# Edge count of a graph layer: compares over 750 (destination, source block) pairs and a final turn by TensorE, in place of compares over all 1250 sources

## The chip, the cores and the metric

The kernel runs on one core of a Trainium2 chip. The metric is device time in microseconds (us) of one launch. Three runs of the kernel before took 2452.61, 2454.36 and 2455.51 us, median 2454.36 us. The core has five engines that matter here, each with its own instruction queue: PE (TensorE, matmuls, with its weight loads shown as PEld), DVE (VectorE), ACT (ScalarE), POOL (GpSimd) and SP (which issues DMAs). They meet at semaphores.

## The reference, cut to what matters

The program is four layers on 1250 nodes with 512 features: graph attention, mixture of experts, message passing, a spline network. Only the first is touched:

```python
K = (x @ Wk + bk).reshape(N, HEADS, DK)          # N = 1250, HEADS = 8, DK = 32
Q = (x @ Wq + bq).reshape(N, HEADS, DK)
V = (x @ Wv + bv).reshape(N, HEADS, DV)
att = jnp.exp(jnp.einsum('ehd,ehd->eh', Q[receivers], K[senders]) / sqrt(DK))   # 21250 edges
denom = jax.ops.segment_sum(att, receivers, num_segments=N)
att = att / denom[receivers]
msg = att[:, :, None] * V[senders]
agg = jnp.zeros((N, HEADS, DV), dtype=V.dtype).at[receivers].add(msg)
```

`receivers` and `senders` come from `edge_index = stack([src, dst])`, so the sum runs over each node's outgoing edges. The edges are sorted by `dst`. An edge may occur more than once, so what the layer needs of the graph is a dense matrix count[dst, src], 1250 x 1250: how many edges there are from each source to each destination.

## The kernel before, in words

The kernel is written engine by engine in blocks. A block ends when every engine has come to its end; then the next block's instructions start. Inside a block the order on each engine is the order of the code, and nothing but semaphores ties the engines. No planner is in it.

The first block of `attention` is the one that changes. It does this:

1. DVE makes small tables from the edge lists (`unit_ranges`, lines 199 to 248) while PE computes the node means (line 400). DVE waits there for a maximum over partitions by POOL (line 189). Then DVE centres x (486), ACT squares (451), PE takes the variance (406), ACT and DVE make the scale and apply it (454, 490, 492).
2. PE multiplies the result with Wq, Wk, Wv in 22 pieces, 12 for q and k (line 389) and 10 for v (line 393). ACT and DVE take them out of PSUM (446, 475, 481). Eight pieces come ahead of the count, the others are spread over it (`GROUPS`).
3. The count. The 21250 edges are 170 tiles of 125 edges, in 43 units of 4 tiles (`TU`). The destinations are 10 blocks of 125. For each block b a loop runs over the units that may hold its destinations, with bounds that `block_range` loads from a table at run time. Since a unit can lie in two blocks, the loops make 52 turns in all, 208 tiles. For each tile DVE writes two one-hot matrices in f16:

```python
dve.tensor_scalar(dst1[:, q, :], c.iota16[:, b * B:b * B + B],          # line 502, 125 x 125
                  c.dstF[:, bass.ds(u * TU + q, 1)], None, ALU.is_equal)
ins = dve.tensor_scalar(src1[:, q, :], c.iota16[:, 0:N],                # line 504, 125 x 1250
                        c.srcF[:, bass.ds(u * TU + q, 1)], None, ALU.is_equal)
```

PE multiplies dst1 (stationary) with src1 (moving, three matmuls of 512, 512 and 226 columns, line 427) and sums in PSUM over all tiles of the block, between matmuls with zeros that open and close the sum (420, 432). DVE may be one loop turn ahead of PE. At the end of a block ACT copies the 125 x 1250 sums into `count[:, b, :]` and takes their row sums on the way (`deg`, line 460), and PE goes on to the next block only when that is done (`s_out`).

The next block of the program loads q and k from memory (`stack`, on SP) and starts the scores (line 593). `count` is used there by DVE. A later stage (message passing, lines 1343 to 1449) has already an edge loop of the kind that the change uses here: windows over destinations per unit, `unit_windows` (lines 119 to 121) for the table loads, one-hots by ACT (1444, 1449), a sum by PE (1357) that DVE adds to an accumulator (1399). Line 1222 is a matmul of f32 data as the stationary operand with an identity as the moving one.

## Time and profile before

| what | us |
|---|---|
| median of three runs | 2454.36 |
| the profiled execution | 2449.78 |
| its span (first to last instruction) | 2448.1 |
| PE busy in the span | 2158.8 |
| DVE busy | 1373.3 |
| ACT busy | 1051.4 |
| POOL busy | 575.8 |
| first compare of the count starts at | 76.92 |
| last count copy by ACT starts at | 269.05 |
| first score matmul of the next block at | 284.72 |

How to read it: all starts are us from the span's start. A row of a timeline has the start, the length, the engine, the line of the code, the operation, the names of what it writes and reads, the shape, how many instructions were merged into the row, and in brackets how long the engine had been idle before it and who ended that. The length of an instruction runs a little into the next one's on DVE and PE, which are pipelined, so the distance between starts is shorter than the length. A f32 matmul shows as two matmul instructions, each with a weight load of its own. DVEq and PEldq are instructions that an engine's sequencer does by itself (loads of a register, arithmetic on it, branches).

### The profile page before, as it was taken

The page shows a single profiled execution, that of the slowest core. Times are in us where ns is not written, and L with a number is a line of the kernel's source. Part 1 is how long each engine was busy: PE and PEld are TensorE (multiplying, and loading weights), DVE is VectorE, ACT ScalarE, POOL GpSimd, SP SyncE. Part 2 cuts the span into 40 slices and gives each one's busy share as a digit, 9 for nine tenths or more (in the row PEclk, how much of TensorE's full clock was granted, in tenths as well). Part 3 has the DMA queues.
Part 4 walks back from the last instruction along what each step waited for, and adds up shares of the span by engine and source line. Part 5 has one row for each costly group of instructions (what it writes and reads, how often), then busy time and mean ns, then how long its engine had stood idle before and what let it go on. Part 6 is the DMA issues. An engine that isn't in the chain of part 4 may idle for free. (4 is left out here: it accounts for less than half of the span.)

```text
span 2448.1 us, 36182 instructions
## 1 busy us (share of the span) xinstructions
PE 2158.8 (88%) x12773; PEld 1662.3 (68%) x12773; DVE 1373.3 (56%) x1922; ACT 1051.4 (43%) x1402; POOL 575.8 (24%) x527
## 2 busy tenths in 40 slices
PE   6898699778949999999995786999999995899998
PEld 2455344355539999999994735999855553799998
DVE  5577577434226666666660053555412127999997
ACT  1100266121016666666660014777601114766665
POOL 1000100001742222222215606888500004000000
PEclk9999899878969999999997898999999997999999
DMA  2100340112038888888874525788520003000001
GB/s 104 51 8 0 84 99 18 36 56 94 2 95 267 283 279 281 282 285 283 282 241 129 148 70 159 205 202 205 152 91 0 0 0 155 1 1 1 0 0 43
DMA packets 111369, 287.13 MB, mean 117 GB/s; under 512 B 48070, under 2 KB 55221, under 8 KB 101536
## 3 DMA queue, kind: packets, MB, share of 16 engines
q1 hardware_dynamic: 45536, 195.78, 24.4%
q0 software_dynamic: 65728, 89.97, 13.9%
q8 instruction: 63, 1.03, 0.2%
q14 instruction: 42, 0.34, 0.0%
HBM read 239.16 MB, written 43.65 MB: 116 GB/s over the span
## 5 line engine op out<-in xcount | busy, mean ns | idle before, releaser
L1832 PE MATMUL ps<-ft,kw 128*128 128x125 f32 x2880 | 342.1, 279 | 37.4 <-DVE ft L1757 24.3
L1832 PEld LDWEIGHTS ps<-ft,kw 128*128 128x128 f32 x2880 | 330.0, 193 | 51.6 <-DVE ft L1757 31.1
L1142 DVE TENSOR_TENSOR wl<-wexp,wh 128x2048 fp32r<-128x2048 f32 (+1 forms) x128 | 225.0, 1759 | 162.3 <-ACT wh L1064 162.3
L1016 PE MATMUL ps<-xh,wh 128*128 128x234 f32 x1024 | 287.6, 281 | 2.2 <-DVE xl L1155 2.2
L1016 PE MATMUL ps<-xh,wl 128*128 128x234 f32 x1024 | 283.3, 277 | 0.0
L1016 PE MATMUL ps<-xl,wh 128*128 128x234 f32 x1024 | 282.9, 276 | 0.0
L1326 POOL DMA_INDIRECT pg<-prows,srcI x170 | 216.6, 1274 | 54.6 <-issue 39.5
L1064 ACT ACTIVATE wh<-wexp 128x2048 fp32r<-128x2048 f32 (+1 forms) x128 | 190.9, 1492 | 63.2 <-DVE gates L1135 63.2
L1016 PEld LDWEIGHTS ps<-xh,wh 128*128 128x128 f32 x1024 | 197.7, 193 | 2.6 <-DVE xl L1155 2.6
L1016 PEld LDWEIGHTS ps<-xh,wl 128*128 128x128 f32 x1024 | 198.4, 194 | 0.0
L1016 PEld LDWEIGHTS ps<-xl,wh 128*128 128x128 f32 x1024 | 198.1, 193 | 0.0
L1357 PEld LDWEIGHTS ps<-ehot,msg 125*128 125x128 f32 x1360 | 160.9, 195 | 11.7 <-issue 5.9
L1357 PE MATMUL ps<-ehot,msg 125*128 125x125 f32 x1360 | 161.8, 278 | 6.9 <-ACT ehot L1449 5.7
L983 POOL DMA_INDIRECT xg<-nrows,idn x128 | 141.1, 1102 | 76.5 <-POOL idn L979 53.7
L1781 ACT ACTIVATE ksq<-ksrc,kn 128x750 f32<-128x750 f32 (+2 forms) x144 | 116.5, 813 | 97.4 <-DVE cube L1740 97.4
L427 PE MATMUL ps<-src,dst 125*125 125x512 f16 (+1 forms) x624 | 133.7, 357 | 17.9 <-DVE src L504 17.9
L1701 POOL COPY ksrc<-nT 128x500 f32<-128x500 f32 (+1 forms) x10 | 10.7, 1074 | 518.9 <-SPq L1692 279.5
L427 PEld LDWEIGHTS ps<-src,dst 125*125 125x125 f16 x624 | 76.1, 141 | 74.8 <-DVE src L504 44.4
L1740 DVE SCALAR_TENSOR_TENSOR cube<-ksrc,kn,ksq 128x750 f32<-128x750 f32 (+2 forms) x144 | 124.7, 880 | 2.6 <-ACT ksq L1781 0.9
L1435 ACT ACTIVATE msg<-epre 125x1024 f32<-125x1024 f32 x85 | 89.8, 1057 | 61.0 <-DVE epre L1389 56.6
L504 DVE TENSOR_SCALAR src<-iota,srcF 125x1250 f16<-125x1250 f16 x208 | 112.6, 541 | 0.0
L1389 DVE TENSOR_TENSOR epre<-ps,pg 125x1024 f32<-125x1024 f32 x85 | 102.3, 1221 | 11.3 <-DMA pg<-prows,srcI 8.6
(256 smaller groups left out, 4009.9 us busy)
## 6 DMA issues: line engine op xcount, KB each, us to landing
wexp<-wexp_d SPq DMA_DIRECT2D x64, 1024.0 KB, 7.3
wexp<-wexp_d SPq DMA_DIRECT2D x64, 512.0 KB, 6.6
yrows<-y SPq DMA_DIRECT2D x64, 468.0 KB
attr<-attr_d SPq DMA_DIRECT2D x42, 250.0 KB, 5.1
kw<-kw_d SPq DMA_DIRECT2D x2, 4608.0 KB, 19.0
qs<-qk SPq DMA_DIRECT2D x32, 156.2 KB, 5.5
ks<-qk SPq DMA_DIRECT2D x32, 156.2 KB, 5.7
qk<-qkhl SPq DMA_DIRECT2D x16, 256.0 KB, 2.4
```

The source lines that it names most:

```text
L427: mm = pe.matmul(c.psf[0:B, a:a + w], dst1[:, q, :], src1[:, q, a:a + w], start=False, stop=False, skip_group_check=True)
L504: ins = dve.tensor_scalar(src1[:, q, :], c.iota16[:, 0:N], c.srcF[:, bass.ds(u * TU + q, 1)], None, ALU.is_equal)
L983: pool.indirect_dma_start(xg[:, q, h, :], None, d["nrows"], bass.IndirectOffsetOnAxis(ap=idn[:, q, h:h + 1], axis=0)).then_inc(s_g[q], 16)
L1016: mm = pe.matmul(c.ps[:, 2 + 2 * s + w, m * CAP:m * CAP + CAP], lhs[:, s, a:a + P], rhs[:, s, k, :], start=(k == 0 and n == 0), stop=(k == ...
L1064: act.activation(wh[:, s, part], wexp[:, s, part], ACT.Copy).then_inc(to, 1)
L1142: dve.tensor_tensor(wl[:, s, part], wexp[:, s, part], wh[:, s, part].bitcast(F32), ALU.subtract)\
L1326: pool.indirect_dma_start(pg[:, p % 4, t % 2, :], None, d["prows"], bass.IndirectOffsetOnAxis(ap=c.srcI[:, t:t + 1], axis=0)).then_inc(s_g ...
L1357: mm = pe.matmul(c.ps[:, ACC, m * W:m * W + W], msg[:, u % 2, q, m * P:m * P + P], hot[:, q, :], start=(q == 0), stop=(q == last))
L1389: dve.tensor_tensor(pre[:, p % 3, :, :], c.ps[0:B, at:at + 2, :], pg[:, p % 4, :, :], ALU.add)\
L1740: dve.scalar_tensor_tensor(cube[:, j % RT, cs], x, kcol(NEG, j), sq[:, j % 2, cs], ALU.add, ALU.mult).then_inc(s_cube, 1)
L1781: act.activation(sq[:, j % 2, cs], x, ACT.Square, bias=kcol(NEG, j)).then_inc(s_sq, 1)
L1832: mm = pe.matmul(out[:, m * B:m * B + B], w[:, k, f, m * P:m * P + P], ft[:, f % RF, a:a + B], start=False, stop=False, skip_group_check=True)
```

## The change

The count is made the other way round. Instead of a sum per block of destinations over all 1250 sources, each unit, now of 8 tiles (`TC`, 22 units, the last with 2 tiles), makes its own small sum and adds it to a table.

The table `pairs` has 125 rows, the place of the source in its block of 125, and 12500 columns, one for each pair (destination, source block), at 10 times the destination plus the block. For each tile DVE writes one one-hot over 750 pairs (75 destinations from the unit's first one, 10 blocks), `row1`; ACT writes the one-hot of the place, `low1`, by a square and a relu of a distance. PE multiplies them (512 and 238 columns) and sums over the unit's 8 tiles; DVE adds the 125 x 750 sum to the table at an offset known at run time. If a unit's destinations reach over more than 75, the loop goes round again for the next 75, for which DVE lowers `rel` by 750; for the given edges every one of the 22 units reaches over 13 to 62 destinations, so that each loop goes round once. At the end PE turns the table: for each of the 10 destination blocks and each of the 10 source blocks a f32 matmul has 125 columns of the table, 10 elements apart, as its stationary operand and the identity as its moving one (12 matmuls a block, since two of them are cut at a PSUM bank's edge). ACT copies the result over the same place, `count`, with the row sums as before.

The table `pairs` is set to zero by POOL (125 x 13250, f32). The v and q/k pieces that lay between blocks now lie one by one ahead of units 1 to 14 on PE, and behind their adds on DVE. In `unit_ranges` the bounds of the blocks are gone; new are the block and place of each edge's source (11 small DVE instructions of 125 x 176 ahead of the wait for POOL) and a second set of window tables. The attention itself and all later stages are the same.

```diff
+TC = 8
+UC = -(-T // TC)
+WC, SH10 = 75, NB
+CW = WC * SH10
+NWC = -(-N // WC)
...
-def block_range(c, eng, b):
-
-
-    lo = eng.value_load(c.tab[0:1, b:b + 1], min_val=0, max_val=U - 1)
-    hi = eng.value_load(c.tab[0:1, NB + b:NB + b + 1], min_val=1, max_val=U)
-    off = eng.value_load(c.tab[0:1, 2 * NB + b:2 * NB + b + 1], min_val=0, max_val=U * NB + U)
-    return lo, hi, off
+def count_windows(c, eng, u):
+
+    base = eng.value_load(c.ctab[0:1, u:u + 1], min_val=0, max_val=N - 1)
+    count = eng.value_load(c.ctab[0:1, UC + u:UC + u + 1], min_val=1, max_val=NWC)
+    before = eng.value_load(c.ctab[0:1, 2 * UC + u:2 * UC + u + 1], min_val=0, max_val=UC * NWC)
+    return base, count, before
...
+        then(dve.tensor_scalar(sh[:, :], srcF[:, :], float(B), None, ALU.is_ge))
+        for j in range(2, NB):
+            then(dve.scalar_tensor_tensor(sh[:, :], srcF[:, :], float(j * B), sh[:, :], ALU.is_ge, ALU.add))
+        then(dve.scalar_tensor_tensor(c.slN[:, :], sh[:, :], float(B), srcF[:, :], ALU.mult, ALU.subtract))
+        then(dve.scalar_tensor_tensor(sh[:, :], dstF[:, :], float(SH10), sh[:, :], ALU.mult, ALU.add))
...
+        first = hi_c[:, 1, :].rearrange("p (u o) -> p u o", o=1).broadcast_to([B, UC, TC])
+        then(dve.scalar_tensor_tensor(by_unit(c.rel[:, :]), first, float(SH10), by_unit(sh[:, :]), ALU.mult, ALU.add))
+
+        def windows(table, units, top, neg, steps, hits, number):
+
+            a = lambda t: t[0:1, 0:units]
+            then(dve.tensor_scalar(a(low), neg, -1.0, None, ALU.mult))
+            then(dve.tensor_tensor(a(reach), top, a(low), ALU.subtract))
+            spread = a(reach).rearrange("p (o u) -> p o u", o=1).broadcast_to([1, number, units])
+            then(dve.tensor_tensor(hits[:, :, :], spread, steps[:, :, :], ALU.is_ge))
+            then(dve.tensor_reduce(a(cnt), hits[:, :, :].rearrange("p b u -> p u b"), AX_X, ALU.add))
+            then(dve.memset(a(one), 1.0))
+            then(dve.tensor_tensor_scan(a(pre), a(one), a(cnt), 0.0, ALU.mult, ALU.add))
+            then(dve.tensor_tensor(a(pre), a(pre), a(cnt), ALU.subtract))
+            dve.tensor_copy(table[:, 0:units], a(low))
+            dve.tensor_copy(table[:, units:2 * units], a(cnt))
+            then(dve.tensor_copy(table[:, 2 * units:], a(pre)))
+
+        windows(c.ctab, UC, hi_c[0:1, 0, :], hi_c[0:1, 1, :], thrc, cc, NWC)
+        windows(c.utab, U, hi_u[0:1, 0, :], hi_u[0:1, 1, :], thr, c1, NB)
...
-        count = sm("count", [B, NB, N], F32)
+        table = sm("pairs", [B, N * SH10 + CW], F32)
+        count = table[:, 0:N * SH10].rearrange("p (b n) -> p b n", b=NB)
...
-        sizes = (8, 2, 2, 2, 2, 2, 1, 1, 1, 1)
-        GROUPS = [range(sum(sizes[:b]), sum(sizes[:b + 1])) for b in range(NB)]
+        GROUPS = [range(0, 8)] + [range(7 + u, 8 + u) for u in range(1, 15)] + [range(0)] * (UC - 15)
...
+            low1 = sf("low1", [B, 2, TC, B], F16)
+            row1 = sf("row1", [B, TC, CW], F16)
+            dist = sf("fdist", [B, TC, B], F32)
...
+                pool.memset(table[:, :], 0.0).then_inc(s_zero, 1)
...
+                pe.wait_ge(s_tab, 1)
+                for u in range(UC):
+                    for r in GROUPS[u]:
+                        piece(r)
+                    base, number, n = count_windows(c, pe, u)
+                    last = len(tiles_of(u)) - 1
+                    pe.wait_ge(s_low, u + 1)
+                    with pe.Fori(0, number) as k:
+                        for q in range(last + 1):
+                            if q % 2 == 0:
+                                pe.wait_ge(s_row, n * full + k * halves(u) + q // 2 + 1)
+                            for a, w in ((0, 512), (512, CW - 512)):
+                                mm = pe.matmul(c.psf[0:B, a:a + w], low1[:, u % 2, q, :], row1[:, q, a:a + w],
+                                               start=(q == 0), stop=(q == last))
+                        mm.then_inc(s_seg, 1)
+                pe.wait_ge(s_ev, len(PIECES))
+                pe.wait_ge(s_add, n + number)
                 for b in range(NB):
-                    for r in GROUPS[b]:
-                        piece(r)
-                    if b == 0:
-                        pe.wait_ge(s_tab, 1)
-                    else:
-                        pe.wait_ge(s_out, b)
-                    lo, hi, off = block_range(c, pe, b)
-                    for a, w in SPANS:
-                        pe.matmul(c.psf[0:B, a:a + w], c.zero16[0:1, 0:B], c.zero16[0:1, 0:w],
-                                  start=True, stop=False, skip_group_check=True)
-                    with pe.Fori(lo, hi) as u:
-                        for h in range(TU // 2):
-                            pe.wait_ge(s_hot, (u + off) * 2 + h + 1)
-                            for q in (2 * h, 2 * h + 1):
-                                for a, w in SPANS:
-                                    mm = pe.matmul(c.psf[0:B, a:a + w], dst1[:, q, :],
-                                                   src1[:, q, a:a + w], start=False, stop=False,
-                                                   skip_group_check=True)
-                            mm.then_inc(s_free, 1)
-                    for a, w in SPANS:
-                        mm = pe.matmul(c.psf[0:B, a:a + w], c.zero16[0:1, 0:B], c.zero16[0:1, 0:w],
-                                       start=False, stop=True, skip_group_check=True)
-                    mm.then_inc(s_full, 1)
+                    if b >= 2:
+                        pe.wait_ge(s_out, b - 1)
+                    for g in range(SH10):
+                        nodes = table[:, b * N:b * N + N].rearrange("p (n g) -> p g n", g=SH10)[:, g, :]
+                        for a, end in parts(g):
+                            mm = pe.matmul(turned(b)[:, a:end], nodes, c.ident[0:B, a - g * B:end - g * B],
+                                           start=True, stop=True, skip_group_check=True)
+                    mm.then_inc(s_turn, 1)
...
+                act.wait_ge(s_tab, 1)
+                for u in range(UC):
+                    m = len(tiles_of(u))
+                    if u:
+                        act.wait_ge(s_low, u)
+                    for q in range(m):
+                        ins = act.activation(dist[:, q, :], c.iota16[:, 0:B], ACT.Square,
+                                             bias=c.slN[:, u * TC + q:u * TC + q + 1])
+                    ins.then_inc(s_dist, 1)
+                    act.wait_ge(s_dist, u + 1)
+                    if u >= 2:
+                        done = act.value_load(c.ctab[0:1, 2 * UC + u - 1:2 * UC + u], min_val=1, max_val=UC * NWC)
+                        act.wait_ge(s_seg, done)
+                    act.activation(low1[:, u % 2, 0:m, :], dist[:, 0:m, :], ACT.Relu, scale=-1.0,
+                                   bias=c.one[0:B, 0:1]).then_inc(s_low, 1)
+                    for r in GROUPS[u]:
+                        high(r)
                 for b in range(NB):
-                    for r in GROUPS[b]:
-                        high(r)
-                    act.wait_ge(s_full, b + 1)
-                    act.activation(count[:, b, :], tile_sum(c, 0, B), ACT.Copy,
-                                   accum_out=c.deg[:, b:b + 1]).then_inc(s_out, 1)
+                    act.wait_ge(s_turn, b + 1)
+                    act.activation(count[:, b, :], turned(b), ACT.Copy, accum_out=c.deg[:, b:b + 1]).then_inc(s_out, 1)
...
-                for r in GROUPS[0]:
-                    evict(r)
-                for b in range(NB):
-                    lo, hi, off = block_range(c, dve, b)
-                    with dve.Fori(lo, hi) as u:
-                        for h in range(TU // 2):
-                            dve.wait_ge(s_free, (u + off) * 2 + h + 1)
-                            for q in (2 * h, 2 * h + 1):
-                                dve.tensor_scalar(dst1[:, q, :], c.iota16[:, b * B:b * B + B],
-                                                  c.dstF[:, bass.ds(u * TU + q, 1)], None, ALU.is_equal)
-                                ins = dve.tensor_scalar(src1[:, q, :], c.iota16[:, 0:N],
-                                                        c.srcF[:, bass.ds(u * TU + q, 1)], None, ALU.is_equal)
-                            ins.then_inc(s_hot, 1)
-                    if b:
-                        for r in GROUPS[b]:
+                dve.wait_ge(s_zero, 1)
+                for u in range(UC):
+                    if u == 0:
+                        for r in GROUPS[0]:
+                            evict(r)
+                    base, number, n = count_windows(c, dve, u)
+                    tiles = tiles_of(u)
+                    with dve.Fori(0, number) as k:
+                        dve.wait_ge(s_next, n + k + 1)
+                        for q, t in enumerate(tiles):
+                            ins = dve.tensor_scalar(row1[:, q, :], c.iota16[:, 0:CW], c.rel[:, t:t + 1], None,
+                                                    ALU.is_equal)
+                            if q % 2:
+                                ins.then_inc(s_row, 1)
+                        dve.wait_ge(s_row, n * full + (k + 1) * halves(u))
+                        cols = c.rel[:, tiles[0]:tiles[-1] + 1]
+                        dve.tensor_scalar(cols, cols, -float(CW), None, ALU.add).then_inc(s_next, 1)
+                        dve.wait_ge(s_seg, n + k + 1)
+                        at = table[:, bass.ds(c.nc.s_assert_within((base + k * WC) * SH10, 0, N * SH10 - SH10), CW)]
+                        dve.tensor_tensor(at, at, c.psf[0:B, 0:CW], ALU.add).then_inc(s_add, 1)
+                    if u:
+                        for r in GROUPS[u]:
                             evict(r)
```

Where the instructions stand now, without times. First DVE, the count's loop in the kernel before, from its entry (`tab` is the table of block bounds, `dst` and `src` the one-hots):

```order
L113 TENSOR_LOAD tab
L113 ISA x2
L498 UNCONDITIONAL_BRANCH
L498 ISA
L502 ISA
L502 TENSOR_SCALAR dst<-iota,dstF 125x125
L504 REGISTER_ALU
L504 TENSOR_SCALAR src<-iota,srcF 125x1250
```

and the same place of the changed kernel, one whole unit and the table loads of the next one (`row` is the one-hot over pairs, `rel` the edges' pair numbers, `pairs` the table):

```order
L528 UNCONDITIONAL_BRANCH
L528 ISA
L531 TENSOR_SCALAR row<-iota,rel 125x750 x8
L535 ISA
L537 TENSOR_SCALAR rel<-rel 125x8
L539 ISA x2
L540 ISA
L540 TENSOR_TENSOR pairs<-pairs,ps 125x750
L528 REGISTER_ALU
L528 COMPARE_AND_BRANCH
L115 TENSOR_LOAD ctab
L115 ISA x2
```

What moved: two compares a tile became one without register work ahead of it, and an add to the table that waits for PE now stands at the end of every unit, ahead of the next unit's table loads (three, of which the first is shown).

Second PE, a loop turn of the kernel before with its end (`zero` closes the sum in PSUM):

```order
L424 REGISTER_ALU
L427 MATMUL ps<-src,dst 125x512 x2
L427 MATMUL ps<-src,dst 125x226
L427 MATMUL ps<-src,dst 125x512 x2
L427 MATMUL ps<-src,dst 125x226
L422 REGISTER_ALU
L422 COMPARE_AND_BRANCH
L432 MATMUL ps<-zero 125x512 x2
L432 MATMUL ps<-zero 125x226
```

and of the changed kernel the last unit's two tiles and the first of the ten blocks of the turn:

```order
L434 MATMUL ps<-row,low 125x512
L434 MATMUL ps<-row,low 125x238
L429 REGISTER_ALU
L429 COMPARE_AND_BRANCH
L438 REGISTER_ALU
L445 MATMUL ps<-ident,pairs 125x125 x4
L445 MATMUL ps<-ident,pairs 125x12
L445 MATMUL ps<-ident,pairs 125x113
L445 MATMUL ps<-ident,pairs 125x125 x3
L445 MATMUL ps<-ident,pairs 125x24
L445 MATMUL ps<-ident,pairs 125x101
```

What moved: the zero matmuls are gone, a tile has two matmuls instead of three, and 120 f32 matmuls (10 blocks of 12) stand behind the last unit.

## Rows read from the trace of the kernel before

**Rows 1.** The page, busy us with share of the span and instructions.

```profile
PE 2158.8 (88%) x12773; PEld 1662.3 (68%) x12773; DVE 1373.3 (56%) x1922; ACT 1051.4 (43%) x1402; POOL 575.8 (24%) x527
```

**Rows 2.** Busy time by stretches: us, PE, PEld, DVE, ACT, POOL, PEclk, DMA share, GB/s.

```profile
76.00:271.00 195.00, 171.24 (x793) 102.46 (x793) 138.43 (x430) 15.20 (x25) 0.00 (x0) 0.97 0.02 7
271.00:285.00 14.00, 0.28 (x1) 0.31 (x2) 0.00 (x0) 0.90 (x1) 6.63 (x3) 0.58 0.99 212
```

**Rows 3.** Waits from 76 to 271: total us, times, longest us.

```profile
DVE dst L502 <- PE ps L427: 52.0, 54, 3.9
```

**Rows 4.** The large compares from 76 to 271: busy us, mean ns, idle before.

```profile
L504 DVE TENSOR_SCALAR src<-iota,srcF 125x1250 f16<-125x1250 f16 x208 | 112.6, 541 | 0.0
```

**Rows 5.** Timeline of DVE: the first compare, and across a block's end.

```profile
76.92 0.26 DVE L502 TENSOR_SCALAR dst<-iota,dstF 125x125 f16<-125x125 f16 x1 [2.05 <-issue]
...
247.24 0.26 DVE L502 TENSOR_SCALAR dst<-iota,dstF 125x125 f16<-125x125 f16 x1
247.41 0.54 DVE L504 TENSOR_SCALAR src<-iota,srcF 125x1250 f16<-125x1250 f16 x1
247.86 0.25 DVE L502 TENSOR_SCALAR dst<-iota,dstF 125x125 f16<-125x125 f16 x1
...
248.48 0.41 DVE L481 TENSOR_TENSOR vs<-ps,par 125x256 f32<-125x256 f32 x1
249.97 0.26 DVE L502 TENSOR_SCALAR dst<-iota,dstF 125x125 f16<-125x125 f16 x1 [1.08 <-PE ps L427]
```

**Rows 6.** Lines 498 and 111 there: ns minimum, median, maximum, first and last start.

```profile
L498 DVEq ALU_OP  x2: 40/40/40, 247.6 to 250.9; - x2
...
L111 DVEq TENSOR_LOAD <-tab x1: 316/316/316, 247.8 to 247.8; - x1
```

**Rows 7.** Timeline of PE in the count.

```profile
193.38 0.73 PE L420 MATMUL ps<-zero 1*125 1x512 f16 x3 [1.40 <-issue]
194.04 5.07 PE L427 MATMUL ps<-src,dst 125*125 125x512 f16 x18
...
233.30 2.35 PE L427 MATMUL ps<-src,dst 125*125 125x512 f16 x12
```

**Rows 8.** Timeline of DVE in the tables ahead of the mean.

```profile
17.56 0.50 DVE L211 TENSOR_REDUCE acc<-acc 1x86 f32<-1x344 f32 x1 [11.17 <-POOL acc L189]
...
22.06 0.59 DVE L224 TENSOR_REDUCE acc<-acc 1x10 f32<-1x430 f32 x1
...
25.60 0.18 DVE L238 TENSOR_SCALAR acc<-acc 1x43 f32<-1x43 f32 x1
...
26.66 0.91 DVE L242 TENSOR_REDUCE acc<-acc 1x43 f32<-1x430 f32 x1
...
28.88 2.29 DVE L486 TENSOR_TENSOR nT<-xT,ps 128x2048 f32<-128x2048 f32 x1 [0.26 <-DVE utab L248]
```

**Rows 9.** Timeline of PE at line 1222, identity times f32 data.

```profile
1337.06 7.25 PE L1222 MATMUL ps<-ident,part 125*128 125x125 f32 x48 [3.79 <-DMA part<-yrows,kidx]
1345.81 5.62 PE L1222 MATMUL ps<-ident,part 125*128 125x125 f32 x48 [1.49 <-DMA part<-yrows,kidx]
...
1364.34 7.25 PE L1222 MATMUL ps<-ident,part 125*128 125x125 f32 x48 [2.13 <-DMA part<-yrows,kidx]
```

**Rows 10.** The message passing stage: a sum by PE and the add behind it.

```profile
1508.94 3.73 PE L1357 MATMUL ps<-ehot,msg 125*128 125x125 f32 x32
...
1513.14 0.68 DVE L1399 TENSOR_TENSOR ST<-ST,ps 128x500 f32 x1 [2.78 <-PE ps L1357]
```

**Rows 11.** Timeline of ACT, one-hots of that stage, and the last count copy.

```profile
269.05 1.21 ACT L460 ACTIVATE count<-ps 125x1250 f32<-125x1250 f32 x1 [17.14 <-PE ps L432]
...
1512.56 1.27 ACT L1444 ACTIVATE edist<-iota,dstN 125x125 f32 x4 [0.59 <-issue]
1513.86 0.72 ACT L1449 ACTIVATE ehot<-edist,one 125x500 f32<-125x500 f32 x1
```

**Rows 12.** POOL's memset at line 1321: ns minimum, median, maximum, first and last start.

```profile
L1321 POOL MEMSET ST<- x1: 4681/4681/4681, 1478.3 to 1478.3; 128x5500 f32 x1
```

More of the change, by code:

```diff
@@ L197, in then @@
             dve.wait_ge(s_step, done[0])
-        dve.memset(c.dstF[:, :], -1.0)
-        dve.memset(c.srcF[:, :], -1.0)
+        dve.memset(dstF[:, :], -1.0)
+        dve.memset(srcF[:, :], 0.0)
         dve.memset(c.dstN[:, :], 1.0)
@@ L229, in dve_part @@
-        for b in range(1, NB):
-            a = 2 * NB + b
-            then(dve.tensor_tensor(tabf[:, a:a + 1], tabf[:, a - 1:a], cnt[:, b - 1:b], ALU.add))
-        then(dve.tensor_tensor(tabf[:, 2 * NB:], tabf[:, 2 * NB:], lo[:, :], ALU.subtract))
-        then(dve.tensor_copy(tabf[:, 0:NB], lo[:, :]))
-        then(dve.tensor_copy(tabf[:, NB:2 * NB], hi[:, :]))
-        then(dve.tensor_copy(c.tab[:, :], tabf[:, :]))
-        top, low = hi_u[0:1, 0, :], hi_u[0:1, 1, :]
-        then(dve.tensor_scalar(ublo[:, :], low, -1.0, None, ALU.mult))
@@ L347, in attention @@
             hl = sf("qkhl", [P, HL, 2, 512], F32R)
[L348 to L352 removed]
+            low1 = sf("low1", [B, 2, TC, B], F16)
+            row1 = sf("row1", [B, TC, CW], F16)
+            dist = sf("fdist", [B, TC, B], F32)
+            s_wqkv, s_mean, s_cent, s_sq, s_var, s_std, s_rstd, s_norm, s_mm, s_hi, s_ev, s_tab, s_dist, \
+                s_low, s_row, s_seg, s_add, s_next, s_zero, s_turn, s_out = (c.sem("fr_" + n) for n in (
+                    "wqkv", "mean", "cent", "sq", "var", "std", "rstd", "norm", "mm", "hi", "ev", "tab", "dist", "low",
+                    "row", "seg", "add", "next", "zero", "turn", "out"))
             s_st = [c.sem(f"fr_st{i}") for i in range(HL)]
```

80 lines of the change are left out of this document (32 added, 48 removed).

## The prediction

> **What bounds the kernel now.** I went from the page's busy shares to a table by stretches, then to the waits, and last to timelines of single engines in the stretch that changes. PE is busy for 88% of the span [rows 1], but the change touches only the first 285 us, so that share says little. In the stretch of the count, 76 to 271, PE is busy for 171 of 195 us and DVE for 138 [rows 2]. Behind it the program has 14 us in which PE has next to nothing, because the next block's loads begin only when this block is over [rows 2]. So whatever end the count stage has, the rest of the program hangs on it one for one, and a reader can treat the stage's last instruction as the end that counts. It is ACT's last copy, 269.05 to 270.3 [rows 11].
>
> Inside the stage two engines share the work. DVE spends 0.17 us from a small compare to the large one and 0.45 from the large to the next small one (247.24, 247.41, 247.86) [rows 5], 0.62 a tile, and 208 tiles [rows 4] make 129 us; DVE's idle time ahead of its compares is put down to PE, 52 us [rows 3], part of it the loop's own turn. PE takes a unit of four tiles, 12 matmuls, in 2.35 us when nothing holds it (233.30) [rows 7], 0.59 a tile. The two alternate closely, and each block end adds a copy by ACT that PE waits for: PE stands idle 1.40 us ahead of line 420 [rows 7]. The stage is thus some 193 us (76.92 to 270.3) for 52 loop turns and 10 ends.
>
> **The change, part by part.**
>
> *The tables ahead of the mean.* DVE waits for POOL until 17.56, and then its own chain runs to 28.88, where the centring starts [rows 8]; PE is done with the mean before that, so this chain sets the start of everything. The 11 new instructions on 125 x 176 stand ahead of the wait, in 11.17 us of idle time [rows 8]; they cost nothing. Behind it the chain was 11.3 us. New: the reduction of 86 again (0.53), one of 125 x 352 (0.55, as the 0.50 of 344 elements), one of 176 elements for `rel` (0.3), a first window table with 374 elements where the old one has 430 (2.95 by the 3.28 from 25.60 to 28.88), and the old one (3.28). That is 7.6 us, 3.7 less. The first compare moves from 76.92 [rows 5] to 73.2, since pieces and evictions between are unchanged. Bounds: 3 to 4.5 us.
>
> *POOL's memset.* 5500 elements take 4.68 us [rows 12], so 13250 take 11.3; begun at 17.5, where DVE's wait for POOL ends [rows 8], they are over at 29, and the first add is at 77. Hidden, with 48 us to spare.
>
> *A unit: the compares and the sum.* A compare of 1250 and one of 125 take 0.45 and 0.17 us of DVE, so 0.25 ns an element, and one of 750 takes 0.33. Each pair of tiles frees PE. PE's tile is 1250 columns in 0.59 us now, 750 in 0.35. The two are about equal. From a unit's first compare: the first pair is ready at 0.33 + 0.41 + 0.06 = 0.8, then PE's 8 tiles take 2.8, and 0.2 goes into drain and waits: 3.8 us. Bounds 3.5 (DVE alone sets it) to 4.3 (a wait shown at each of four pairs).
>
> *A unit: the add and the next start.* This is serial and new. The add waits for the unit's last matmul. In the stage that has the like, PE's group ends at 1512.67 and the add starts at 1513.14, 0.47 later, with two waits and an address to work out [rows 10]; here one wait fewer, I take 0.25 (bounds 0.1 and 0.47). Behind the add come the loop's end and three table loads: in the trace of before the loop's last ALU operation is at 247.6, the first load at 247.8 [rows 6], the next compare at 249.97 [rows 5], 2.35 us in all. Before, this was hidden, since DVE was a turn ahead of PE and its queue still held a compare and an eviction (248.48) [rows 5]. Now the loads begin only when the add has been issued, and the add itself (0.94 us for 750 elements, by the 0.68 for 500 [rows 10] and about one ns for each more) and the eviction (0.41) run beside them. So a unit costs 3.8 + 0.25 + 2.35 = 6.4 us. Evictions are free, and so are the pieces on PE: 2 us right behind the sum, in a hole of 3.4.
>
> *ACT.* Four squares take 1.27 us and a relu of 500 0.72 [rows 11], so 8 squares and a relu of 1000 some 3.6 to 3.9 with a table load, against 6.4 a unit, and one unit ahead by the double buffer. It costs nothing.
>
> *The clock.* The granted clock of PE falls to its lower level (1.2 GHz) where PE has pauses: at line 1222 a group of 48 takes 5.62 us after a pause of 1.49, and 7.25 after pauses of 3.79 and 2.13 [rows 9], 1.63 more. In the count itself 18 matmuls took 5.07 us after a pause of 1.40 [rows 7]. From unit 15 on no piece fills the hole and PE pauses 3.4 us in every 6.4. I charge 1.65 for each of units 15 to 20, and 1.6 for the first unit, which is slow in before too. Units 1 to 14, with 1.4 to 1.8 of pause, I leave warm. Bounds: 0 for all of them, and 14 x 1.65 = 23 more.
>
> *The turn.* 120 f32 matmuls are 240 instructions, each with its weight load. The same operation, data as the stationary operand and identity as the moving one, takes 5.62 / 48 = 0.117 us [rows 9] where the data are contiguous. Here its 125 columns lie 40 bytes apart. No PE row of before shows that. The nearest row is DVE's: a reduction of 430 contiguous f32 takes 0.59 us and one of 430 that lie 172 bytes apart 0.91 [rows 8]. It is not the number of results, for 344 elements with 86 results take 0.50 [rows 8]. With 0.14 of fixed cost (0.59 at 1.04 ns each) the strided read is 1.79 ns an element. 125 of these are 0.224 us, twice what a load has now, and a weight load that long can't hide behind a matmul of 125 columns. Ends: 240 x 0.117 = 28.1 us and 240 x 0.224 = 53.8. I take the upper one, since the slowdown is shown on reads of the same memory and PE asks for elements faster than DVE. ACT's copies (1.3 each against 5.4 a block) hide but for the last one, 1.4.
>
> The Trainium skill speaks against the change here: "SBUF — State Buffer", section "Door 1: The DMA port swizzle", says that accesses that leave a 16-byte line each time pay a penalty, so that four f32 is as far as one strides for free. The trace agrees for DVE, 1.79 against 1.04 ns. The other way points "TensorE: Matmul & The Clock Gate", section "LDWEIGHTS (loading the stationary operand)": a load takes its number of columns divided by 1.2 GHz, 0.104 us for 125, with no term for the stride; line 1222's 0.117 agrees for contiguous data, and by it the turn would stay at the lower end.
>
> *The sum.* First compare 73.2; unit 0 3.8 + 1.6 = 78.6; units 1 to 14 14 x 6.4 = 168.2; units 15 to 20 6 x 8.05 = 216.5; unit 21 with two tiles 2.6 + 0.8 + 1.5 = 221.4; last add 1.3, 222.7; turn 53.8, 276.5; last copy 1.4, 277.9. Before it was 270.3, so the stage ends 7.6 us later. The profiled execution would go from 2449.8 to 2457.4; it lies 4.6 below the median of the runs, which goes from 2454.4 to 2462.
>
> **The rivals.**
>
> *A: the stride is free on PE.* Then the turn is 28.1 + 1.6 (it starts at the low clock) and the stage ends at 253.8, 16.5 us earlier: 2438. For it: 170 tiles in place of 208, and one compare where there were two; the only row of this operation on PE shows 0.117. Against: rows 8. This is the case of a clear gain.
>
> *B: the stride costs, but PE's clock stays high from unit 15 on.* 9.9 us less than my sum: 2452, no difference. For it: the clock held through most of the count, 0.97 [rows 2]. Against: pauses of 3.4 us, after which line 1222 was slow each time.
>
> *C: the clock falls in units 1 to 14 too.* PE then needs 1.65 more in each, 23 in all: 2485 with the stride's cost, 2461 without. For it: the 5.07 us after a pause of only 1.40 [rows 7]. Against: 1.49 without a loss [rows 9]. It decides by how the clock answers to the 1.4 to 1.8 us of pause behind each piece, which the two rows leave open.
>
> The other side for me is A (faster). It decides by the weight load alone: 222.7 + 1.4 + 240 loads reach 270.3 at 0.193 us a load, a gain of 4.9 us at 0.172 and a loss of 4.9 at 0.213.
>
> **How the numbers follow.** I give my forecast 0.56, A 0.30, B 0.08, C 0.06. Within 0.2%, 4.9 us, is what a measurement of this kernel can't tell from no change. My forecast has 7.6 us with an own range of 2454 to 2472 (a unit at 6.1 to 6.8 is minus 6 to plus 8), so some three quarters of it are slower and nearly all the rest is the same; A is faster but for a sliver; B is the same or a bit slower; C slower mostly. Faster 0.32, same 0.20, slower 0.48. The range goes down into A until 2435 and up to 2474.
>
> **What would show it.** Right: first compare near 73; 22 groups of compares about 6.4 us apart, 8 in the last seven full ones, with the table loads of DVE between add and compare; weight loads of the turn starting 0.22 us apart; the turn 54 us long; ACT's last copy near 277. Wrong: turn loads 0.12 apart (A), a granted clock of 1.00 from unit 15 on (B), groups over 7.5 us apart from the start (C), or compares that begin less than 2 us behind the add, by which my serial term would be too large.

## The result and the profile after

| | before | after |
|---|---|---|
| median us | 2453.49 (4 runs, 2452.43 to 2455.51) | 2475.97 (4 runs, 2469.93 to 2481.02) |
| profiled execution | 2449.78 | 2469.93 |
| its span | 2448.1 | 2468.2 |
| end of ACT's last count copy | 270.3 | 287.1 |

The change makes the kernel slower, by a little and clear of the spread: ratio 1.009, 95% interval 1.0063 to 1.0116. I had forecast 2462.0 in a range up to 2474. The direction held; the time is out of the range by 2 us. Two single executions are left out of all ratios, one of the kernel before at 5631.01 us and one of a kernel below at 9319.67 us; nothing recorded says what held them.

The page still says that PE is nearly all of the span, as in [rows 1]:

```profile
PE 2138.6 (87%) x12669; PEld 1678.7 (68%) x12669; DVE 1334.2 (54%) x1719; ACT 1126.8 (46%) x1594; POOL 587.3 (24%) x528
```

PE and DVE are busy for less time than before and the kernel is slower, so the loss isn't in the amount of their work but in when it can be done. Timelines of DVE (first four rows) and POOL (last two) in the tables ahead of the mean, which answer to [rows 8]; the columns are those of the rows ahead of the prediction:

```profile
17.81 0.34 DVE L229 SCALAR_TENSOR_TENSOR rel<-acc 125x176 f32<-125x176 f32 x1
18.18 11.74 DVE L234 TENSOR_SCALAR acc<-acc 1x22 f32<-1x22 f32 x1
29.96 0.17 DVE L235 TENSOR_TENSOR acc<-acc 1x22 f32<-1x22 f32 x1
...
35.86 5.49 DVE L513 TENSOR_TENSOR nT<-xT,ps 128x2048 f32<-128x2048 f32 x3 [0.26 <-DVE utab L244]
```

```profile
16.50 11.22 POOL L373 MEMSET pairs<- 125x13250 f32 x1
27.58 2.31 POOL L374 MEMSET vs<- 125x2560 f32 x1
```

An operation on 22 numbers took 11.74 us. It ends at 29.92, and POOL's second memset ends at 29.89. No semaphore ties the two; the hold doesn't show as idle time but as the length of the instruction, so no view of waits lists it. Ahead of it two reductions and line 229 ran at their usual length beside the same memset. The centring, at 28.88 in [rows 8], starts at 35.86.

A unit in the middle of the count, timeline of DVE (against [rows 5]), and DVE's table loads there with ns minimum, median, maximum, first and last start (against [rows 6]):

```profile
156.41 2.70 DVE L531 TENSOR_SCALAR row<-iota,rel 125x750 f16<-125x750 f16 x8 [0.97 <-issue]
...
160.43 0.94 DVE L540 TENSOR_TENSOR pairs<-pairs,ps 125x750 f32 x1 [1.11 <-PE ps L434]
161.28 0.42 DVE L508 TENSOR_TENSOR vs<-ps,par 125x256 f32<-125x256 f32 x1
162.69 1.39 DVE L531 TENSOR_SCALAR row<-iota,rel 125x750 f16<-125x750 f16 x4 [0.99 <-issue]
```

```profile
L115 DVEq TENSOR_LOAD <-ctab x1: 309/309/309, 160.6 to 160.6; - x1
```

```profile
L117 DVEq TENSOR_LOAD <-ctab x2: 297/305/313, 155.6 to 161.9; - x2
```

From first compare to add 4.02 us, from add to the next compare 2.26, a unit 6.28. The first load (160.6) comes behind the add's issue and the third at 161.9. PE from unit 14 to unit 17, and its turn, which has no counterpart before:

```profile
176.04 2.81 PE L434 MATMUL ps<-row,low 125*125 125x512 f16 x16 [1.74 <-DVE row L531]
182.29 2.81 PE L434 MATMUL ps<-row,low 125*125 125x512 f16 x16 [3.44 <-DVE row L531]
188.54 5.26 PE L434 MATMUL ps<-row,low 125*125 125x512 f16 x16 [3.44 <-DVE row L531]
197.21 4.44 PE L434 MATMUL ps<-row,low 125*125 125x512 f16 x16 [3.41 <-DVE row L531]
...
232.52 53.26 PE L445 MATMUL ps<-ident,pairs 125*125 125x125 f32 x240 [1.40 <-DVE pairs L540]
```

```profile
L445 PEld LDWEIGHTS ps<-ident,pairs x240: 298/315/321, 232.5 to 285.3; 125*125 125x125 f32 x120
```

After two pauses of 3.44 us a group costs 4.2 to 5.3 us in place of 2.81; the granted clock is 1.00 from 150 to 176 and 0.70 from 188 to 230. The turn's 240 loads start (285.3 - 232.5) / 239 = 0.221 us apart, nearly twice the 0.117 of [rows 9]. ACT's last copy answers to the first of [rows 11]:

```profile
285.81 1.21 ACT L488 ACTIVATE pairs<-ps 125x1250 f32<-125x1250 f32 x1 [3.89 <-PE ps L445]
```

Of the span's 20.1 us, 16.8 stand at this copy's end. The other 3.3 lie behind it, where nothing was changed: 2181.1 us from there to the end, against 2177.8. In the profiles of the experiments the same stretch takes 2178.9 to 2184.8, so before's profiled execution was one of its shortest, and the 3.3 lie within what unchanged code varies by.

### The profile page after: what moved, and what is told of

Read it like the earlier page. It is cut to its first block and busy times, and to the rows that moved or that the text cites. A ratio compares the mean times of both kernels' runs of the same rounds, so it can differ in the third digit from the quotient of the medians.

```text
span 2468.2 us, 35717 instructions
## 1 busy us (share of the span) xinstructions
PE 2138.6 (87%) x12669; PEld 1678.7 (68%) x12669; DVE 1334.2 (54%) x1719; ACT 1126.8 (46%) x1594; POOL 587.3 (24%) x528
## 5 line engine op out<-in xcount | busy, mean ns | idle before, releaser
L1360 POOL DMA_INDIRECT pg<-prows,srcI x170 | 216.5, 1274 | 53.1 <-issue 39.5
L1391 PEld LDWEIGHTS ps<-ehot,msg 125*128 125x128 f32 x1360 | 159.7, 193 | 11.6 <-issue 5.8
L1391 PE MATMUL ps<-ehot,msg 125*128 125x125 f32 x1360 | 160.6, 277 | 6.6 <-ACT ehot L1483 5.4
L1017 POOL DMA_INDIRECT xg<-nrows,idn x128 | 141.3, 1104 | 76.5 <-POOL idn L1013 53.8
L434 PE MATMUL ps<-row,low 125*125 125x512 f16 x340 | 73.3, 378 | 54.3 <-DVE row L531 54.3
L1126 ACT ACTIVATE hh<-he 128x468 fp32r<-128x468 f32 x64 | 38.1, 595 | 155.9 <-DVE he L1196 155.9
L1552 PE MATMUL ps<-nT,whh 128*128 128x512 f32 (+1 forms) x288 | 104.7, 512 | 1.7 <-DVE aT L1609 1.7
## 6 DMA issues: line engine op xcount, KB each, us to landing
kw<-kw_d SPq DMA_DIRECT2D x2, 4608.0 KB, 20.1
```

What stands on the lines that cost most here:

```text
L1017: pool.indirect_dma_start(xg[:, q, h, :], None, d["nrows"], bass.IndirectOffsetOnAxis(ap=idn[:, q, h:h + 1], axis=0)).then_inc(s_g[q], 16)
L1360: pool.indirect_dma_start(pg[:, p % 4, t % 2, :], None, d["prows"], bass.IndirectOffsetOnAxis(ap=c.srcI[:, t:t + 1], axis=0)).then_inc(s_g ...
L1391: mm = pe.matmul(c.ps[:, ACC, m * W:m * W + W], msg[:, u % 2, q, m * P:m * P + P], hot[:, q, :], start=(q == 0), stop=(q == last))
L1552: mm = pe.matmul(c.psf[:, at + a:at + a + w], lhs, rhs[:, a:a + w], start=(t == 0), stop=(t == len(terms) - 1))
```

## The experiments

Theories on the missing 10 us ahead of the first compare, and on each term of the sum. Medians are compared with runs of the kernel before made beside them (2454 us).

**Theory M from both sides: the memset moved, and the memset alone.** In the changed kernel POOL waits until DVE's tables are done:

```diff
+                pool.wait_ge(s_tab, 1)
                 pool.memset(table[:, :], 0.0).then_inc(s_zero, 1)
```

> The changed kernel, with POOL's two memsets (the pair table and vs) held back until DVE has finished the tables ahead of the mean. Theory M (a simple DVE operation, here the tensor_scalar of 22 elements at line 234 that took 11.74 us, cannot run while POOL's memset does): that operation takes 0.2 us, the first compare moves from 83.5 to about 72.5, and the time falls by 11 to 12 us, to about 2464. Rival F (the 11.7 us are something else that stands at that place, a fetch of instructions or a semaphore): line 234 still takes 11 us and the time stays within 2 us.

2461.76 us (9 runs, 2458.33 to 2466.13), ratio 1.003 (1.002 to 1.004). The timeline of DVE, and POOL's row:

```profile
18.31 0.17 DVE L234 TENSOR_SCALAR acc<-acc 1x22 f32<-1x22 f32 x1
...
24.45 5.50 DVE L514 TENSOR_TENSOR nT<-xT,ps 128x2048 f32<-128x2048 f32 x3 [0.26 <-DVE utab L244]
...
73.16 2.69 DVE L532 TENSOR_SCALAR row<-iota,rel 125x750 f16<-125x750 f16 x8 [1.91 <-issue]
```

```profile
24.30 11.14 POOL L374 MEMSET pairs<- 125x13250 f32 x1 [7.54 <-DVEq L494]
```

The tensor_scalar is back at 0.17 us, and the centring, a tensor_tensor, takes 5.50 beside the memset as without it. The first compare starts at 73.16, 10.3 us earlier, and the loss against before is 7.5 us. Of the 10.3 the profile keeps 6.4 at ACT's last copy (280.7 against 287.1), for here unit 15 is slow too, and unit 0 slower (5.26 us against 4.45):

```profile
172.82 5.26 PE L435 MATMUL ps<-row,low 125*125 125x512 f16 x16 [3.44 <-DVE row L532]
```

The kernel before with a memset of its 12500 counts, which ACT's copies overwrite, put ahead of POOL's other one:

```diff
+                pool.memset(count[:, :, :], 0.0).then_inc(s_zero, 1)
                 pool.memset(vs[:, :, :, DH:], 1.0)
```

> The kernel before with one thing added: POOL sets the 125 x 12500 count buffer to zero ahead of vs, at the place where the changed kernel sets its table. ACT waits for it ahead of its first copy, 60 us later. Theory M: the first simple DVE operation behind the wait for POOL (line 222, a tensor_scalar of 10 elements at 21.2) is held until both memsets are over at about 30.5, so the first centring starts near 38 instead of 28.9 and the time grows by 8 to 10 us. Rival F: nothing changes, since the tables' code is that of before.

2463.86 us, ratio 1.0046 (1.0029 to 1.0062). DVE, then POOL:

```profile
19.69 0.59 DVE L221 TENSOR_REDUCE acc<-acc 1x10 f32<-1x430 f32 x1
20.31 8.95 DVE L222 TENSOR_SCALAR acc<-acc 1x10 f32<-1x10 f32 x1
29.30 0.59 DVE L223 SCALAR_TENSOR_TENSOR acc<-acc 1x430 f32<-1x430 f32 x1
```

```profile
26.93 2.31 POOL L363 MEMSET vs<- 125x2560 f32 x1
```

Six operations ran unhindered beside the memset, which began at 16.48; the seventh, the first tensor_scalar, was held until 29.26, 0.02 after the end of POOL's second memset. This alone costs the old kernel 9.6 us.

**Theory S: the stride of the turn.** The table in f16 and by source block, so that a weight load reads 125 neighbours, with the add doing the rearranging from PSUM:

```diff
-                        nodes = table[:, b * N:b * N + N].rearrange("p (n g) -> p g n", g=SH10)[:, g, :]
+                        nodes = table[:, g, b * B:b * B + B]
...
-                        dve.tensor_tensor(at, at, c.psf[0:B, 0:CW], ALU.add).then_inc(s_add, 1)
+                        dve.tensor_tensor(at, at, c.psf[0:B, 0:CW].rearrange("p (n g) -> p g n", g=SH10),
+                                          ALU.add).then_inc(s_add, 1)
```

> The changed kernel with a table in f16 and in another order, source block first, so that the turn reads 125 neighbouring columns; the add reads PSUM 10 elements apart instead. The turn then has 120 f16 matmuls instead of 240 f32 instructions. Theory S (the stride of 40 bytes made a weight load 0.22 us): the turn falls from 53.3 us to 14 to 17, ACT's copies of 1.35 a block set it, and the memset is shorter if f16 is; with 0 to 0.5 us more for each of 22 adds the time falls by 30 to 38 us, to about 2440. Rival G (the turn's 0.22 us an instruction are the price of a f32 matmul whose moving operand is an identity of 125 columns right behind another in a new bank, not of the stride): half of the instructions go, so the turn is 27 us and the time falls by about 25.

2434.81 us, ratio 0.9914 (0.9897 to 0.993), with the memset's hold still in it. The weight loads' row:

```profile
L447 PEld LDWEIGHTS ps<-ident,pairs x120: 181/230/231, 236.9 to 251.0; 125*125 125x125 f16 x120
```

120 loads, 0.118 us apart, 14.6 us for the turn in place of 53.3. Half as many loads would take 53 to 27 us, and neighbours in place of the stride the other 12. The granted clock was 0.50 all through this turn. The add, which now reads PSUM 40 bytes apart, stayed at 0.94 us.

**What a stride costs, and what a memset holds.** PE makes groups of 16 matmuls with the stationary data at growing strides, and DVE one operation at a time beside a memset of 4.26 us by POOL.

> All of the computation is left out; it measures two disputed costs. First PE: 16 f32 matmuls each (32 instructions) with an identity as the moving operand and a stationary operand whose 125 columns lie 1, 2, 3, 4, 5, 6, 8, 10, 16 and 40 elements apart, then the same in f16 with 1, 2, 4, 7, 8, 9, 10, 16 and 40, then f32 with the stride on the moving operand, 1, 4 and 10. Theory S: 3.7 us for a group at stride 1, about 7 from some stride on (the Trainium skill's page SBUF - State Buffer would put it above 4 elements of f32 and 8 of f16). Rival G: all groups the same. Second, POOL sets 125 x 5000 to a constant (about 4.4 us) ten times, and each time DVE starts one operation of 750 elements at once: tensor_tensor, scalar_tensor_tensor, tensor_scalar, copy, reciprocal, memset, tensor_scalar in f16, tensor_tensor in f16, tensor_scalar from PSUM, reduction. Theory M: the tensor_scalar and the copy from SBUF wait for the end of the memset, the operations with two tensor operands and the reduction do not.

Timeline of PE: f32 with strides of 1, 2, 3, 4 and 10 elements, then f16 with 1, 4, 7 and 8:

```profile
42.63 3.65 PE L1955 MATMUL ps<-ident,data 125*125 125x125 f32 x32
46.12 3.86 PE L1957 MATMUL ps<-ident,data 125*125 125x125 f32 x32
49.82 5.61 PE L1959 MATMUL ps<-ident,data 125*125 125x125 f32 x32
55.26 7.49 PE L1961 MATMUL ps<-ident,data 125*125 125x125 f32 x32
...
83.90 7.20 PE L1969 MATMUL ps<-ident,data 125*125 125x125 f32 x32
...
107.89 1.91 PE L1975 MATMUL ps<-id,half 125*125 125x125 f16 x16
...
111.31 2.00 PE L1979 MATMUL ps<-id,half 125*125 125x125 f16 x16
113.15 3.41 PE L1981 MATMUL ps<-id,half 125*125 125x125 f16 x16
116.35 3.87 PE L1983 MATMUL ps<-id,half 125*125 125x125 f16 x16
```

Read the distances between starts: f32 3.49, 3.70, 5.44, 7.32 us, and 7.04 at 10; f16 3.20 at 7 against 1.84 at 4. Twice the time from 16 bytes on and no more at 40. The clock isn't the cause: it was granted at 1.00 in all f32 groups up to 16 elements, and at 0.50 in f16 with 1 element (1.71 us) and with 8 (3.67); in f16 with 4 and 7 it was 0.85 and 0.83. At 160 bytes f32 took 10.08 us, at a granted clock of 0.69, so that what the stride has in this one stays open. With the stride on the moving operand instead, 4 elements cost as much: 7.12 us at 1.00. DVE beside the memset:

```profile
159.39 0.94 DVE L1929 SCALAR_TENSOR_TENSOR b<-a 125x750 f32<-125x750 f32 x1 [3.45 <-POOL flag L1912]
163.81 4.50 DVE L1930 TENSOR_SCALAR b<-a 125x750 f32<-125x750 f32 x1 [3.48 <-POOL flag L1912]
168.56 4.50 DVE L1931 COPY b<-a 125x750 f32<-125x750 f32 x1 [0.26 <-POOL flag L1912]
...
191.83 0.94 DVE L1936 TENSOR_SCALAR b<-ps 125x750 f32<-125x750 f32 x1 [3.87 <-POOL flag L1912]
```

Tensor_scalar (f32 and f16) and copy from SBUF are held; a source in PSUM, two inputs, a reduction and a memset are not, nor is a reciprocal: its 4.84 us are its own by an estimate from the 3.35 us of 512 elements in the kernel (4.9 for 750).

**Theory K: is it the kind of operation, in the kernel itself?** The memset stays early. The tensor_scalar and the casts of the tables become operations with two inputs:

```diff
-            then(dve.tensor_scalar(a(low), neg, -1.0, None, ALU.mult))
+            then(dve.scalar_tensor_tensor(a(low), neg, -1.0, neg, ALU.mult, ALU.max))
...
-            dve.tensor_copy(table[:, 0:units], a(low))
+            dve.scalar_tensor_tensor(table[:, 0:units], a(low), 1.0, a(low), ALU.mult, ALU.max)
```

> The changed kernel with POOL's memset where it is, but with the one tensor_scalar and the three casts of each window table written as scalar_tensor_tensor, an operation with two inputs (value times one, maximum with itself: the same numbers). Theory K (the memset holds only some kinds of DVE's operations: of those beside POOL's memset in the measurement by itself, tensor_scalar and copy waited for 3.6 us, scalar_tensor_tensor and tensor_tensor not at all): no row of the chain is longer than 1 us, the first compare starts at 73 us as with the late memset, and the time is about 2462 us. Rival H (the memset holds DVE whatever the operation, since this one comes in the chain and not alone, or holds operands of one partition): the first scalar_tensor_tensor of the table takes some 11.7 us, first compare at 83 us, about 2476 us.

2466.12 us (2462.45 to 2468.88), ratio 1.0054 (1.0037 to 1.007):

```profile
17.61 0.17 DVE L234 SCALAR_TENSOR_TENSOR acc<-acc 1x22 f32<-1x22 f32 x1
...
72.21 2.70 DVE L531 TENSOR_SCALAR row<-iota,rel 125x750 f16<-125x750 f16 x8 [1.89 <-issue]
```

Theory K holds: the same numbers by another operation, beside a running memset of 11.22 us, are not held. That the median is 4 us over the late memset's, and not the same, I can't explain beyond the spread of the runs, which overlap.

**Would smaller memsets let DVE in?** The memset cut into eight:

```diff
-                pool.memset(table[:, :], 0.0).then_inc(s_zero, 1)
+                for i in range(8):
+                    ins = pool.memset(table[:, cuts[i]:cuts[i + 1]], 0.0)
+                ins.then_inc(s_zero, 1)
```

> The changed kernel with the memset of pairs cut into eight, some 1.4 us each, in the same place. Theory P (DVE's instruction waits for the memset in flight and gets in between two of them): the first tensor_scalar of the tables takes at most 1.5 us, the casts and the second table's tensor_scalar up to 1.5 us each, 3 to 5 us in all, first compare at 76 to 78 us, about 2467 us. Rival W (POOL keeps DVE out as long as its memsets follow each other): the tensor_scalar still takes 11.7 us, first compare at 83 us, about 2476 us.

2469.62 us (2467.34 to 2471.72), ratio 1.0065 (1.0048 to 1.0082). DVE, then POOL:

```profile
18.02 12.02 DVE L234 TENSOR_SCALAR acc<-acc 1x22 f32<-1x22 f32 x1
```

```profile
16.34 11.49 POOL L375 MEMSET pairs<- 125x1562 f32 x8
27.70 2.31 POOL L377 MEMSET vs<- 125x2560 f32 x1
```

My theory P fell. DVE's instruction began in the second memset and was held over it and the seven behind it, until 30.04; POOL's last ended at 30.01. The first compare stayed at 83.33. The median is still 6 us under the changed kernel's, with runs that overlap; the hold doesn't account for that.

**Theory L: the table loads between add and compare.** They are issued behind the compares of the unit before:

```diff
-                    base, number, n = count_windows(c, dve, u)
+                    base, number, n = following
...
+                        if u + 1 < UC:
+                            following = count_windows(c, dve, u + 1)
```

> The changed kernel with DVE's three table loads for the next unit issued right behind the eight compares of the unit before, beside which DVE waits for PE anyway, and not between the add and the next compare. Theory L (the loads are in series with the add, some 1.3 us of the 2.35 us between add and next first compare): units go from 6.27 us to 5.0 to 5.3 us at PE's full clock, 21 units give back 20 to 27 us, and the time is about 2450 us. Rival Q (DVE's queue is read ahead and the loads are hidden already, the time between is the eviction and the handshake): units stay at 6.2 us and the time within 3 us of the changed kernel's. A fall of PE's pause per unit may also leave fewer units at PE's low clock, which would add up to 1.65 us for each one.

2440.51 us, ratio 0.9942 (0.9925 to 0.9958), faster than the kernel before. Timeline of DVE:

```profile
153.27 0.94 DVE L543 TENSOR_TENSOR pairs<-pairs,ps 125x750 f32 x1 [1.11 <-PE ps L434]
154.12 0.42 DVE L508 TENSOR_TENSOR vs<-ps,par 125x256 f32<-125x256 f32 x1
154.46 2.69 DVE L532 TENSOR_SCALAR row<-iota,rel 125x750 f16<-125x750 f16 x8
```

From add to compare 1.19 us, not 2.26, a unit 5.19. Measured 35 us by the medians, more than the 27 of my expectation (28 by the profiled executions); first compare to turn is 29.1 shorter in the profiles (149.1 to 120.0). Of it 22 are the loads, and the rest PE's clock: units 0 and 2 ran at 2.81 us, and the slow units came 6.5 us apart in place of 8.2, with groups mostly of 4.4 us, not 5.3. The last 6 us of the 35 lie in the spread of the changed kernel. One pause by itself doesn't decide about the clock: here a group of 4.44 us stands behind 2.05 us of pause, while unit 4 of the changed kernel ran at 2.81 behind 2.31, with a piece of 1.70 us ahead of the pause.

**Theory C: the clock.** Matmuls that nobody reads, into a free bank of PSUM, behind each unit's sum:

```diff
+                    for _ in range(6 if u < 14 else 14):
+                        pe.matmul(c.psf[0:B, 1024:1536], c.iota16[:, 0:B], c.iota16[:, 0:512], start=True, stop=True,
+                                  skip_group_check=True)
```

> The changed kernel with matmuls that nobody reads (125x512 f16, into a PSUM bank that is free here) behind the sum of each unit, 6 of them in the first fourteen units and 14 later, so that PE doesn't pause. Theory C (units 15 to 21 run at 4.4 to 5.3 us for PE's group and not 2.81 us because PE paused and its clock fell): groups stay at 2.81 us, 7 to 9 units give back 1.65 us each, 12 to 15 us in all, about 2462 us, and the runs lie closer together than the 11 us of the changed kernel. Rival D (the clock falls for a reason that more work of PE doesn't remove, or the fill delays the next unit's sum): the time stays at 2470 to 2480 us, or grows by the part of the fill that lies ahead of the next sum.

2462.09 us, ratio 1.0034 (1.0024 to 1.0045). Eight of nine runs lie within 5.1 us. PE in the stretch where the changed kernel is slow:

```profile
188.07 2.81 PE L434 MATMUL ps<-row,low 125*125 125x512 f16 x16 [0.41 <-DVE row L534]
190.71 3.18 PE L438 MATMUL ps<-iota 125*125 125x512 f16 x14
194.28 2.81 PE L434 MATMUL ps<-row,low 125*125 125x512 f16 x16 [0.39 <-DVE row L534]
```

All units but the first run at 2.81 us, and the granted clock is 1.00 from 160 to 200, where the changed kernel has 0.88. 14 us come back by the medians, for work that is of no use; in the profiles first compare to turn is 10.4 shorter. The turn itself takes 53.1 us here too, though it starts from the high clock.

**All together.** Late memset, f16 turn and loads ahead:

> POOL's memset behind the distances' start, the turn from f16 with each column beside the next, and the three table loads behind the compares, all in one. If the three causes are independent (theory M 14 us, theory S 41 us, theory L 20 to 27 us): 2476 - 14 - 41 - 22 = about 2400 us, from 2393 to 2410. If loads ahead are worth nothing (rival Q): about 2421 us. If less work of DVE per unit only leaves PE's clock lower in more units, between the two.

2391.6 us, ratio 0.9748 (0.973 to 0.9765). From 2476, less the measured 14, 41 and 35, would be 2386 (my expectation, with 22 for the loads, was 2400). The three are nearly independent. With fewer unread matmuls added (2, and 8 from unit 14 on):

> The version before (memset late, turn from f16, loads ahead) with the matmuls that nobody reads behind each unit's sum, 2 in the first fourteen units and 8 later. Theory C: PE's groups stay at 2.81 us in all units, up to 10 to 15 us less than without, about 2388 us. Rival D: the same time as without, or up to 5 us more for the fill.

2379.33 us, ratio 0.9696 (0.9679 to 0.9712): 75 us less than the kernel before, and the fastest here. In its turn, at a granted clock of 1.00, PE needs 0.90 us a block and ACT 1.19, so ACT's copies bound it now.

## Why the prediction was wrong

| step | predicted | measured |
|---|---|---|
| first compare | 73.2 | 83.45 (73.16 with the memset late) |
| first compare to turn | 149.5 | 149.1 |
| in a unit: to the add, and on to the next compare | 4.05, 2.35 | 4.02, 2.26 |
| a slow unit | 8.05 | 8.2 (188.54 to 229.61, five units) |
| the turn | 53.8 | 53.3 |
| end of the last copy | 277.9 | 287.1 |

The step that failed is "POOL's memset", which ended "Hidden, with 48 us to spare". I compared the memset's end with the first add that needs it, and asked nothing of what POOL and DVE do to each other in between. It cost 11.6 us at line 234, 10.3 at the first compare. With the memset late the first compare is at 73.16, where I had 73.2: of the terms of the sum this is the one that carries the error.

That the median is then 2461.76, beside my 2462.0, is more than the sum can claim, and part of it is luck. In that kernel's profile the last copy ends at 280.7, 2.8 behind my 277.9, since unit 2 was slow too and units 15 to 20 took 8.4 us, not 8.05; the code behind it takes 4.3 us more than in the profile that I started from; and the median lies 2.7 below the profiled execution, where I had put it 4.6 above. These cancel.

Could the trace of before have told me? Not by itself: there the small memset ran from 17.40 to 19.71, and the chain's operations beside it were a reduction and some with two inputs, kinds that aren't held; its first tensor_scalar came at 21.23, and took 0.16 us:

```profile
17.40 2.31 POOL L361 MEMSET vs<- 125x2560 f32 x1
...
21.23 0.16 DVE L222 TENSOR_SCALAR acc<-acc 1x10 f32<-1x10 f32 x1
```

Rows that show no conflict were rows in which none could arise. Here the Trainium skill would have been worth a sentence. "SBUF — State Buffer", section "Who interferes with whom", says that copy, cast and tensor_scalar can take a port pair that DVE shares with GpSimd, an exclusive lock that blocks the other for a whole instruction, and that an operation with two SBUF inputs meets only a GpSimd instruction that reads. Beside a memset, which reads nothing, the probe agrees: 4.50 us for tensor_scalar and copy, 0.94 for two inputs. The split memset goes further than that page: DVE was held over eight instructions of POOL, not one.

The hold is shown for POOL's memsets alone. In the trace of before four tensor_scalars of DVE stand beside tensor_scalars of POOL in a later stage (duration in ns, minimum, median, maximum):

```profile
L1689 POOL TENSOR_SCALAR kw<-kw,kn x8: 2838/3212/3624, 2051.8 to 2073.8; 128x1024 f32<-128x1024 f32 x8
L1689 DVE TENSOR_SCALAR kw<-kw,kn x4: 741/1182/1602, 2051.5 to 2054.4; 128x1024 f32<-128x1024 f32 x4
```

POOL's first runs from 2051.77 to 2055.39, and two of DVE's begin and end inside it (2052.24 to 2053.84, 2053.76 to 2054.50). What makes the difference, POOL's operation or the form of the operands, no run here shows.

The tables' other step was right: 7.6 us from the first reduction to the centring (16.85 to 24.45 with the memset late). Rival A (the stride is free on PE) is out by 0.221 us a load. My 0.224 came from DVE's reads. That the stride costs was right; that the size fits is partly luck, since DVE's elements lay 172 bytes apart and PE's 40, and PE's own group at 160 bytes took 10.08 us where the one at 40 took 7.04. "Door 1: The DMA port swizzle", in the Trainium skill's "SBUF — State Buffer", which I had cited for "four f32 is as far as one strides for free", is too lenient for PE here: the probe has 1.56 times at three elements and 2.1 at four, so the measurement decides. Rival B fell with the slow units 16 to 20, rival C with units 3 to 15 at 2.81 us. The clock's step was right in kind and nearly in size; unit 2 was slow without my having foreseen it, unit 15 was not. So 149.1 meets 149.5 by errors that cancel: one slow unit for another, ordinary units of 6.33 us on the mean (106.31 to 182.29, twelve units) for my 6.4, and slow ones of 8.2 for 8.05. The runs spread by 11 us, where the kernel before had 3 in its four runs and 8 in eleven others; my range moved only the middle and had no such term. The filled kernel's 5.1 us point to the clock as the source, but don't show it.

Left open: 10.3 us of the 14.2 between the medians with the early and the late memset are seen at the first compare, and 6.4 are left of them at the last copy of the two profiles. The changed kernel's profiled execution is the shortest of its four, 6 us under their median, so the rest lies within the spread of these runs. So do the 4 and 6 us noted at the two-input and the split memset kernel.

## What to carry to other kernels

Cover isn't only time: when work is moved to POOL, and a memset above all, go through what DVE runs in that stretch and look at each operation's kind, for a held instruction shows as a long one and in no list of waits. A tensor_scalar or a copy on a handful of numbers can be written with two inputs, or the memset started behind the chain; cutting it into eight didn't help here. Where a loop's end is serial, loads of its next bounds belong behind the previous iteration's issue, and operands for weight loads belong side by side.

## What the hardware showed unexpectedly

- A row of memsets by POOL held DVE's tensor_scalar until the last was over, 12.02 us over eight of them.
- A memset of 13260 f16 took POOL 11.23 us, and one of 13250 f32 11.22: with half the bytes, the same time.
- Weight loads cost double at 16 bytes between columns, in f32 (7.32 us a group for 3.49) and in f16 (3.67 for 1.71), and no more at 40 bytes in f32 (7.04); DVE's add read PSUM 40 bytes apart at no cost (0.94 us both ways).
- 92 more matmuls of 512 columns made the fastest kernel 12 us faster, since PE kept its higher clock.
